# Front of a sequence layer: load buffers of one row, more rows kept, and part of the routing on GpSimd

## What is computed

```
x = x + conv(layernorm(x)) + layernorm(x) * omega        # per channel, over all 4096 positions
x = x + moe(layernorm(x))                                # 4096 tokens of the result, 2 of 8 experts each
```

## Time and profile before

| what | us |
|---|---|
| median of 3 runs (1102.78 to 1105.65) | 1104.19 |
| the profiled execution | 1103.91 |
| its span | 1101.7 |
| busy in it: PE | 889.2 |
| VectorE | 809.6 |
| ScalarE | 764.0 |
| GpSimd | 577.0 |
| front, up to the first matmul of the convolution | 119.6 |
| convolution of `g = 0`, up to about | 376 |

### The profile page before, as it was taken

The page is one execution under the profiler, slowest core; times in us unless marked ns, Lnnn a source line. Parts: engine busy times, 40 slices in busy tenths (PEclk is TensorE's granted clock), DMA queues, the critical chain, the costliest instruction groups (busy, mean ns, idle before and its releaser), DMA issues. The chain is left out here.

```text
span 1101.7 us, 31975 instructions
## 1 busy us (share of the span) xinstructions
PE 889.2 (81%) x11186; PEld 732.8 (67%) x11186; DVE 809.6 (73%) x1350; ACT 764.0 (69%) x1124; POOL 577.0 (52%) x641
## 2 busy tenths in 40 slices
PE   2770588879868878999999999999779888886981
PEld 1540576767757757777777777778657777775771
DVE  7978897988969534567665666766668889796891
ACT  3872698989969744656565565656359989896990
POOL 5445886878855143556566565655554333232330
PEclk9995799999989989999999999999889999899996
DMA  8999999999999989999999888899949999999976
GB/s 301 344 400 364 228 255 223 260 250 287 315 280 307 277 194 281 235 282 283 258 293 221 251 211 240 213 238 241 235 106 277 244 245 264 253 315 296 305 169 153
DMA packets 390535, 286.21 MB, mean 260 GB/s; under 512 B 124784, under 2 KB 338434, under 8 KB 389948
## 3 DMA queue, kind: packets, MB, share of 16 engines
q1 hardware_dynamic: 345980, 211.67, 70.9%
q0 software_dynamic: 17952, 34.42, 15.3%
q10 hardware_dynamic: 26528, 39.14, 10.0%
HBM read 195.57 MB, written 98.77 MB: 267 GB/s over the span
## 5 line engine op out<-in xcount | busy, mean ns | idle before, releaser
L1565 PE MATMUL ps<-xn,wb 128*128 128x128 f32 x2048 | 275.4, 290 | 0.0
L1565 PEld LDWEIGHTS ps<-xn,wb 128*128 128x128 f32 x2048 | 250.3, 200 | 17.3 <-issue 2.8
L622 POOL TENSOR_TENSOR cen<-xb,mean 128x512 f32<-128x512 f32 x128 | 142.3, 1113 | 221.9 <-DVE state L1371 151.0
L1344 DVE TENSOR_TENSOR xn<-cen,rstd 128x1024 f32<-128x1024 f32 x128 | 176.0, 1375 | 43.9 <-POOL cen L622 33.9
L1552 PE MATMUL ps<-xn,near 128*32 128x128 f32 x2048 | 86.5, 288 | 116.5 <-DVE xn L1344 71.9
L1355 DVE TENSOR_TENSOR xb<-xb,ps 128x1024 f32 (+1 forms) x128 | 152.8, 1194 | 9.4 <-PE ps L1577 9.4
L1027 ACT ACTIVATE wb<-wide 32x1024 f32<-32x1024 f32 x126 | 144.5, 1147 | 15.5 <-DMA wide<-taps_d 12.9
L1129 ACT ACTIVATE cen<-ps 128x1024 f32<-128x1024 f32 x110 | 109.5, 1024 | 64.2 <-PE ps L1675 42.0
L1552 PEld LDWEIGHTS ps<-xn,near 128*32 128x32 f32 x2048 | 52.0, 112 | 140.4 <-issue 72.2
L1675 PE MATMUL ps<-carry,wb 64*128 64x256 f32 x1024 | 127.9, 390 | 6.7 <-issue 4.1
L1675 PEld LDWEIGHTS ps<-carry,wb 64*128 64x128 f32 x1024 | 99.8, 191 | 37.2 <-issue 24.4
(11 more groups left out here) (211 smaller groups left out, 1454.1 us busy)
## 6 DMA issues: line engine op xcount, KB each, us to landing
xb<-L_attn_x SPq DMA_DIRECT2D x160, 512.0 KB, 9.2
out<-xb SPq DMA_DIRECT2D x72, 512.0 KB, 6.5
xb<-L_attn_x ACTq DMA_DIRECT2D x128, 256.0 KB
out<-xb SPq DMA_DIRECT2D x88, 256.0 KB, 4.5
wb<-L_ffn_w_B SPq DMA_DIRECT2D x78, 256.0 KB
wide<-taps_d SPq DMA_DIRECT2D x63, 256.0 KB
dk<-decay_d SPq DMA_DIRECT2D x63, 128.0 KB
out<-y_d SPq DMA_DIRECT2D x4, 1536.0 KB
```

What stands on the lines that cost most here:

```text
L622: pool.tensor_tensor(cen[:, k, 0:QB // 2].rearrange("p b r d -> p r b d"), unit_view(pool, g, i, k)[:, :, 0:UC // 2] .rearrange("p r (b d) ...
L1344: dve.tensor_tensor(xn[:, k].rearrange("p (b d) r -> p b d r", d=2), cen[:, k].rearrange("p b r d -> p b d r"), rstd[:, g * P:(g + 1) * P] ...
L1565: ins = pe.matmul(ps[:, QB * k + b, d * P:(d + 1) * P], wb[:, h, k * QB + b, d, :], xn[:, k, 2 * b + d, :], start=(b > 0 and d == 0), stop ...
```

## The change

- **Buffers of one row.** `LR = 1`: still eight buffers, 256 KB each, so 120 loads in SyncE's loop instead of 56. GpSimd copies in pairs of rows (`keep(m)`), and SyncE waits for the pair's copy before it reloads either buffer.
- **More kept.** `KEPT = 128 - 8 * 512 / 128 = 96`: of the first 96 rows GpSimd also copies the channels of tile 1 into the half of `xb` that tile 1 uses; the ring lies in its last 32 rows. In tile 0 SyncE loads only the last 4 of tile 1's 16 pieces; `loads_in` counts that.
- **Tables' store.** The decays are made in the four buffers of `dk` instead of 32 of their own, so ScalarE waits for the store of four blocks before (`s_dec[k]`).
- **Routing.** VectorE keeps 19 steps, put between its statistics in five slices from the ninth row on. Thirty steps go to GpSimd, as 39, since each scan over the 8 experts becomes three shifted additions on a zero-padded row (`padded`, one memset more among the constants). GpSimd has then 75 steps, one or two after each pair from the 13th on.
- **Sends.** None in the front. Units 0 to 56 carry them, two in the units 7, 15, 23, 31, 39, 47 and 55. SyncE's wait for them and its load of the slot table go behind the expert weights and the stores of that block.
- **Statistics.** Five chained steps instead of eight; the division by 512 goes into ScalarE's square root. GpSimd starts centring after the second step. VectorE centres the first unit before it takes the reciprocal.
- **First copy and weights.** GpSimd copies the first pair among the constants. SyncE issues three blocks' weights before it waits for the last copies.

The diff, cut to its core:

```diff
-    LR = 2
+    LR = 1
     LBUF = 8
+    KEPT = P - LBUF * LR * D // P
...
-        loadbuf = xb[:, 1].rearrange("p a b -> p (a b)")[:, D * N:].rearrange("p (k r d) -> p k r d", k=LBUF, r=LR)
-        decays = xb[:, 1].rearrange("p a b -> p (a b)")[:, 0:D * N].rearrange("p (k n d) -> p k n d", k=NK, n=N)
+        loadbuf = xb[:, 1].rearrange("p a b -> p (a b)")[:, KEPT * P:].rearrange("p (k r d) -> p k r d", k=LBUF, r=LR)
+        decays = dk[:].rearrange("p k (n d) -> p k n d", n=N)
+        padded = xn_row[:, 0:5 * 2 * E].rearrange("p (a b) -> p a b", a=5)
...
+        def loads_in(t):
+            return 16 * (PIECES * (t if t < DG else t - 1) - KEPT // PR) if t > 0 else 0
...
+            def keep(m):
+                n, b = 2 * m, 2 * m % LBUF
+                for k in range(2):
+                    pool.wait_ge(s_load[b + k], 16 * (n // LBUF + 1))
+                if n < KEPT:
+                    pool.tensor_copy(xb[:, :, n:n + 2, :],
+                                     loadbuf[:, b:b + 2, 0, 0:2 * P].rearrange("p r (h c) -> p h r c", h=2))\
+                        .then_inc(s_keep, 1)
+                else:
+                    pool.tensor_copy(xb[:, 0, n:n + 2, :], loadbuf[:, b:b + 2, 0, 0:P]).then_inc(s_keep, 1)
...
+            const(pool.memset(padded, 0.0))
+            keep(0)
             const(pool.memset(slot_init, 0.0))
...
+                def scan(dst, a):
+                    yield rt(pool.tensor_tensor(padded[:, 3, E:], padded[:, a, E:], padded[:, a, E - 1:2 * E - 1], ALU.add))
+                    yield rt(pool.tensor_tensor(padded[:, 4, E:], padded[:, 3, E:], padded[:, 3, E - 2:2 * E - 2], ALU.add))
+                    yield rt(pool.tensor_tensor(dst, padded[:, 4, E:], padded[:, 4, E - 4:2 * E - 4], ALU.add))
...
-            for n in range(NL):
-                keep(n)
+            for m in range(1, NL // 2):
+                keep(m)
...
-                if n >= 2 * LBUF:
-                    for _ in range(3):
+                if m >= 3 * LBUF // 2:
+                    for _ in range(1 + m % 2):
                         next(rest, None)
-                if n >= NL - 2 * SENT and n % 2 == 1:
-                    send((n - (NL - 2 * SENT)) // 2)
...
                         if g == 0 and first and k == 1:
+                            pool.wait_ge(s_dv, DV_VAR)
                             clear(1)
-                        if g == 0 and SENT + u < NSEND:
-                            send(SENT + u)
+                        if g == 0:
+                            for c in range(u + u // LEVEL, min(u + 1 + (u + 1) // LEVEL, NSEND)):
+                                send(c)
...
-                    now(sp, read)
+                    now(sp, read, (q - 1) * (LBUF // 2) + k // 2 + 1)
                     wait(sp, s_free, read)
-                    wait(sp, s_keep, read)
+                    wait(sp, s_keep, (q - 1) * (LBUF // 2) + k // 2 + 1)
                     sp.dma_start(loadbuf[:, k], x_rows[:, bass.ds(at, LR), :])
...
+                        if first and g == 0 and j < KEPT // PR:
+                            continue
                         if first and 0 <= j < PIECES:
                             load_tile(g, t + 1, [j])
...
+                wait(act, s_dec[i % WB], 16 * (i // WB))
...
-                yield chain(dve.tensor_tensor(m, st[:, 1, :], st[:, 4, :], ALU.add))
-                yield chain(dve.tensor_scalar(m, m, 0.5, None, ALU.mult))
                 yield chain(dve.tensor_tensor(r, st[:, 1, :], st[:, 4, :], ALU.subtract))
-                yield chain(dve.tensor_tensor(r, r, r, ALU.mult))
-                yield chain(dve.tensor_scalar(r, r, D / 4.0, None, ALU.mult))
+                yield chain(dve.scalar_tensor_tensor(m, r, 0.5, st[:, 4, :], ALU.mult, ALU.add))
+                yield chain(dve.scalar_tensor_tensor(r, r, D / 4.0, r, ALU.mult, ALU.mult))
                 yield chain(dve.tensor_tensor(r, r, st[:, 2, :], ALU.add))
                 yield chain(dve.tensor_tensor(r, r, st[:, 5, :], ALU.add))
-                yield chain(dve.tensor_scalar(v, r, 1.0 / D, None, ALU.mult))
...
             parts = routing()
+            row_stats(1, (0, 1))
             next(parts)
-            row_stats(0, (5, 6, 7))
-            row_stats(1)
+            row_stats(1, (2, 3))
             next(parts)
+            row_stats(1, (4, 5))
+            next(parts)
+            row_stats(1, (6, 7))
+            next(parts)
+            row_stats(2)
+            next(parts)
+            row_stats(3)
             row_stats_rest()
             for _ in statistics(0, stats1):
                 pass
-            dve.wait_ge(s_std, 1)
-            dve.reciprocal(rstd[:, 0:P], rstd[:, 0:P]).then_inc(s_dv, 1)
-            dve.wait_ge(s_dv, DV_STATS)
...
             centre(0, 0, 0)
+            dve.wait_ge(s_std, 1)
+            dve.reciprocal(rstd[:, 0:P], rstd[:, 0:P]).then_inc(s_dv, 1)
+            dve.wait_ge(s_dv, DV_STATS)
             stage(0, 0, 0)
```

More of the change, by code:

```diff
@@ new lines, in routing_rest @@
+                prefix, units = small[:, 1, :], small[:, 2, :]
+                odd, pairs, alone = (padded[:, a, E:] for a in range(3))
+                begin, kept, one, ends, end_slot = (small[:, a, :] for a in range(3, 8))
+                yield rt(pool.tensor_scalar(odd, pairs, -2.0, None, ALU.mult))
+                yield rt(pool.tensor_tensor(odd, odd, units, ALU.add))
+                yield from scan(one, 0)
+                yield rt(pool.tensor_tensor(one, one, odd, ALU.subtract))
+                yield rt(pool.tensor_scalar(one, one, float(NS), None, ALU.is_lt))
@@ new lines, in routing_rest @@
+                yield rt(pool.tensor_tensor(one, one, odd, ALU.mult))
+                yield rt(pool.tensor_tensor(pairs, pairs, odd, ALU.add))
+                yield rt(pool.tensor_tensor(pairs, pairs, one, ALU.subtract))
+                yield from scan(ends, 1)
+                yield rt(pool.tensor_tensor(begin, ends, pairs, ALU.subtract))
+                yield rt(pool.tensor_scalar(kept, ends, float(NP), None, ALU.min))
+                yield rt(pool.tensor_scalar(end_slot, begin, float(NP), None, ALU.min))
@@ L1274, in routing @@
                 rt(dve.tensor_scalar(smalli[:], smalli[:], P.bit_length() - 1, None, ALU.arith_shift_right))
-                prefix, units, pairs, odd, odds, at, one = (small[:, n, :] for n in range(1, 8))
-                rt(dve.tensor_copy(units, smalli[:]))
+                rt(dve.tensor_copy(small[:, 2, :], smalli[:]))
                 rt(dve.tensor_scalar(smalli[:], smalli[:], 1, None, ALU.arith_shift_right))
-                rt(dve.tensor_copy(pairs, smalli[:]))
-                rt(dve.tensor_scalar(odd, pairs, -2.0, None, ALU.mult))
```

148 lines of the change are left out of this document (75 added, 73 removed).

## The result

| what | us |
|---|---|
| median after (4 runs, 1116.49 to 1122.33) | 1119.53 |
| median before, beside it (4 runs, 1102.03 to 1105.65) | 1103.49 |
| ratio, with its 95% interval | 1.0143 (1.0111 to 1.0175) |
| the profiled execution, and its span | 1116.49, 1114.7 |

A forecast was written before the change was run, and what follows sets the result against it. The prediction took the load stream to set the end of the front. Stream -1.9, tail -1.5 and sends +3.1 summed to -0.3 us: 1103.6 for the profiled execution, 1103.9 for the median, range 1098 to 1111.

The forecast's parts named there:

- Start of the stream: Front's head: small stores take about 0.4 us each, SyncE's loop starts at 12.6, first row lands 3.2 us earlier.
- The steady stream: Loads behind row 32: SyncE's floor gives a period of 0.77 us, statistics end at 111.0, 1.9 us earlier.
- Rival 1: Load stream slows with a ring of 8 rows: period 0.85, statistics end at 118.6, total 1111; chance 0.17.
- The tail: Last row statistics to first convolution matmul: five steps at 0.38, 5.2 us against 6.67, 1.5 us earlier.
- The sends: Convolution units with two sends: 1.0 us each in 7, 23 and 55, 0.1 for unit 56; 3.1 us later.
- The prediction's sign: VectorE still waiting after tile 2 for less than 3 us would mean that unit 39's double send is not swallowed.
- Skipped loads of tile 1: Tile 0 of the convolution: twelve of 16 pieces, 6.3 MB, go; worth 0, at best 0.5 us.
- Routing off VectorE: Front: thirty steps, 7.4 us, leave VectorE; worth nothing by themselves where loads set the pace.
- The sum: Whole kernel: -1.9 - 1.5 + 3.1 = -0.3 us, 1103.6 for the profiled execution, 1103.9 for the median.
- The 358 GB/s rule: Front's load stream: at the skill's 358 GB/s the statistics end at 115.4, total 1108; chance 0.03.

The follow-up runs named there:

- e10: Kernel before with five statistics steps, the store of `taps_d` first and the other two small stores behind the second round of loads; ratio 0.9976.
- e1: Changed kernel with 16 load buffers of one row instead of 8, so 64 rows of tile 1 kept; 1110.25 us, ratio 1.0058 to the kernel before.
- e8: Changed kernel with 16 one-row buffers, sends as before the change, GpSimd's centring behind all five statistics steps, small stores moved; ratio 0.9894 to the kernel before.
- e6: Changed kernel with SyncE waiting for the last copies before it issues the weights of blocks 1 to 3; 1096.06 us in one run.
- e5: Changed kernel with GpSimd's first centring waiting for all five statistics steps instead of two; 1099.42 us in one run.
- e4: Changed kernel with the eight moved sends behind the last units of tiles 0, 1 and 2; 1118.51 us, ratio 1.0135 to the kernel before.
- e7: Changed kernel with 16 one-row buffers, and sends and GpSimd's routing pace as before the change; ratio 1.0034 to the kernel before.
- e11: The kernel of e8 again, unchanged, with more runs; ratio 0.9975 to the kernel before.
- e9: Kernel before with only the five-step statistics chain and VectorE's first centring ahead of the reciprocal; ratio 0.999.
- e3: Changed kernel with 4 buffers of two rows, ring still 8 rows, 96 rows kept; 1124.49 us, ratio 1.0203 to the kernel before.
- e2: Changed kernel with 8 buffers of two rows, ring of 16 rows, 64 rows kept; 1110.84 us, ratio 1.0064 to the kernel before.

## Why the prediction was wrong

**Start of the stream: right, and worth less than thought.** Stores of 0.4 us, loop from 12.6 and row 24 at 32.3 were forecast; 0.24 to 0.45, 12.36 and 32.5 came. The head start of 3.4 us was worth little: with only 8 rows in the ring the statistics of 24 rows were done by 33 us, where the kernel before had 31. e10 shows that such a head start buys nothing in the kernel before either. The reading that a queue full of loads makes the stores long holds only in part: with 4 MB of first loads again (e1) they take 0.76 and 3.16, but in e8, where `y_d` follows the store of `taps_d`, it takes 0.36.

**The steady stream: this step failed.** "The ring: eight rows at 0.77 allow 6.2 us from issue to reissue; landing 4.15, copy 0.8 and the other of the pair 0.7 make 5.65, so it holds, barely. I take SyncE's floor". The 4.15 us was the landing of one load into a queue that had just run empty. Under steady traffic half the size takes 5.1 us at the median (33 to 90 us). The measured turn is 8 x 0.843 = 6.7 us; 5.1, the pair's 0.7 to 0.84 and the copy's 0.61 make 6.4 to 6.6 of it, and 0.1 to 0.3 is left for wake-ups. The landing time of a full queue isn't a constant to be taken from elsewhere: it belongs to the bytes in flight (10.0 us in e1, 5.1 here), and with 2 MB in flight the stream no longer reaches its rate (376 GB/s against 397). Of the 9.1 us between the forecast end (111.0) and 120.09, the period makes 95 x (0.843 - 0.77) = 6.9, the issue of row 32 at 33.37 instead of 33.0 0.4, and the rest is the last row: 6.66 us from its issue to the end of its statistics instead of 4.8, most of it by the weights (1.3 in e6). Rival 1 named this mechanism and gave it 0.17; with 5.65 of 6.2 us used, and the 5.65 made from a landing at an empty queue, it should have been the forecast. Its own price, 1111, would still have been short, as it held the tail and the units at their forecast.

**The tail: this step failed.** "Five steps at 0.38 are 1.9 us" left out that the change moves GpSimd's wait from the last step to the second. They took 2.9, and the scaling 1.81 for 1.23. Forecast 5.2, measured 6.76: 1.6 us. With that wait moved back it is 5.57 (e5), of which the scaling is 1.50.

**The sends: mechanism right, count short.** 1.0 us for a double was forecast, 1.1 came in units 7, 23 and 39 and 0.8 in unit 55, and the second send ran at 0.98 as chosen. The reason given for 1.00, that VectorE's addition leaves GpSimd alone, these rows don't test: the send of 172.35 took 1.00 beside the scaling, which reads two SBUF inputs. And unit 39 was not swallowed: VectorE waited 3.75 us for its load after tile 2 instead of 4.05, and unit 48 took 14.27 against 14.40. (The prediction's sign has the sense turned round: had the load swallowed the lateness, the wait would have shrunk to 3.0.) That the load itself moved, since SyncE's transfers start only when the tile before is done, is a reading; this wait is 2.4 to 7.0 us in the other traces, so one trace doesn't show it. And tile ends were not free: units 15 and 16 together +0.6, 47 and 48 +0.8, 31 and 32 nothing; e4 shows the same on a larger scale. Unit 1 lost 0.6 more, with TensorE's granted clock at 0.50 until 132, where before it was at 1.00 from 123 on; unit 2 lost 0.2. In all 6.2 us for 3.1.

**Skipped loads of tile 1: 0, as forecast.** With the eight sends back, the stretch takes 252.1 us (e7) and 250.2 (e11) against 251.3 before and 251.1 in e9, though eight of the 16 pieces are not loaded in it. A gain or loss below 2 us this can't exclude.

**Routing off VectorE: 0, as forecast.** VectorE is idle for loads 14 us in the stream after the change; 7.4 us less work in it is only more waiting. With 16 rows in the ring the statistics end at 111.6 to 113.2 without these steps (e1, e7, e8, e11) and at 111.5 to 112.9 with them (before, e9, e10).

**The sum.** Against the forecast for the profiled execution, 1103.6: +9.1 (stream) + 1.6 (tail) - 0.9 (unit 0's scan comes 2.1 us behind the first matmul, not 3.0) + 3.1 (units) = 1116.5; measured 1116.49. The median of the four runs lies 3.0 us above that execution, which was the fastest. The prediction has no term for the 0.9. It is what GpSimd's early start gives back: VectorE's centring ahead of that scan no longer runs beside GpSimd's (before, then after), and in e5, with the late start, the scan comes 3.85 us behind.

```profile
118.95 1.32 POOL L622 TENSOR_TENSOR cen<-xb,mean 128x512 f32<-128x512 f32 x1
119.23 1.59 DVE L1333 TENSOR_TENSOR cen<-xb,mean 128x512 f32<-128x512 f32 x1
```

```profile
124.40 1.11 POOL L687 TENSOR_TENSOR cen<-xb,mean 128x512 f32<-128x512 f32 x1
...
126.52 0.68 DVE L1377 TENSOR_TENSOR cen<-xb,mean 128x512 f32<-128x512 f32 x1
```

**The 358 GB/s rule.** The stream did slow, and e1 settles whether that was the cause: 397 GB/s as a mean from 33 to 80 us and 398 to 401 in windows of 10 us, with one load of 256 KB after the other. The Trainium skill's figure of about 358 GB/s per core (DMA: Bandwidth & Descriptors, Specifications) isn't a ceiling for this kernel on one core.

**What stays open.** Why the store of `y_d` takes 3.2 us directly behind that of `slot_d` with 16 rows in flight (3.21 before, 3.16 in e1), and 0.36 to 0.45 elsewhere; nothing depends on it here. The 4.9 us by which e3 is slower than the changed kernel with as many rows in the ring was not taken apart; a buffer of two rows that returns as a whole is what differs. Nor were the 2.9 us between e2 and e1, and the share of the longer copy in the turn of a buffer. Keeping 96 rows for tile 1 with a ring of 16 was not tried, since there is no room for both.

## What to carry to other kernels

A ring of buffers has a period of its own: the landing time *under the traffic of the stream*, plus everything until the buffer is released, over the number of buffers; halving the ring to shorten each transfer saves nothing once the bytes in flight are too few for the rate. A wait that is moved forward so that an engine starts earlier can lengthen the chain that it waited for: here 1.2 us, where both then worked on SBUF. Work that hides in a front bound by loads is not free in a loop where that engine is released by another and waited for in turn: a second send cost 1.1 us in each of three units, in full, and 0.8 in a fourth.

## What the runs showed of the hardware

- The same VectorE addition of two 128x128 operands takes 0.38 us alone, 0.38 beside GpSimd's steps of 8 elements, and 1.16 beside GpSimd's subtraction of 128x512; the scaling of 128x1024 takes 1.23 with a send beside it (118.09, before) and 1.81 beside that subtraction. In these rows the instruction that started second was the one that took longer.
- Landing time (median) and rate by bytes in flight, from 33 to 90 us: 2 MB in single rows 5.1 us and 376 GB/s; 4 MB in single rows 10.0 us and 397; 2 MB in pairs 5.7 us and 363; 4 MB in pairs 11.6 us and 397. The DMA share was 1.02 to 1.06 in all four.
- Of the small stores, the first behind a queue with 4 MB of loads takes longer, whichever it is (1.72 us before, 0.76 in e1 and 0.57 in e2 for `slot_d`, 1.71 in e10 and 1.62 in e11 for `taps_d`), and with 2 MB it doesn't (0.24 and 0.25 for `slot_d`).
- With three blocks' weights issued behind it the last load landed in 5.2 to 6.1 us (four traces), without them in 4.3 (e6): here transfers issued later on the same queue took time from an earlier one.
